# Collecting the 256-column side products of the composition at the end of each half of a group

## The reference, cut to what matters

```
x = x + L0(x, W0, b0, coeff, mask)          # x @ W0.T + b0 + coeff * (x @ (2*mask - 1))
x = x + L1(x, weight, ...)                  # x @ w_eff.T, w_eff a quantized 1024x1024 matrix
x = x + L2(x, W2, b2, lora_As, lora_Bs)     # x @ W2.T + b2 + 2 * (x @ A[tok2]) @ B[tok2]
x = x + L3(x, A3, B3)                       # (x @ B3[tok3].T) @ A3[tok3].T
```

## Time and profile before

| | us |
|---|---|
| median of 3 runs | 558.34 |
| profiled execution, its own time | 558.08 |
| span of the profile | 556.0 |
| around the span | 2.1 |
| PE busy | 541.1 |
| DVE busy | 397.4 |
| ACT busy | 330.4 |
| POOL busy | 151.2 |

### The profile page before, as it was taken

How to read it: one execution, slowest core, us unless ns; L and a number is a source line. 1 busy time by engine, 2 the same in 40 slices (tenths; PEclk the granted TensorE clock), 3 DMA queues, 4 the chain that set the end, 5 groups by cost and what they waited for, 6 DMA issues and landing times.

```text
span 556.0 us, 8879 instructions
## 1 busy us (share of the span) xinstructions
PE 541.1 (97%) x2892; PEld 464.4 (84%) x2892; DVE 397.4 (71%) x624; ACT 330.4 (59%) x624; POOL 151.2 (27%) x166
## 2 busy tenths in 40 slices
PE   5999999999998999999999999999999999999997
PEld 4988888888887888888888888888888888888886
DVE  5998898988856886585775767567576667856631
ACT  3777776776646765564565565546557556644620
POOL 2769778987710030021012002102100300210200
PEclk9999999999999999999999999999999999999999
DMA  8766042733686992481393367149138435814302
GB/s 230 242 90 145 21 141 70 238 107 109 122 200 220 280 259 90 150 209 72 129 204 130 132 144 215 59 156 233 56 138 186 154 130 133 227 39 151 75 0 75
DMA packets 138120, 80.07 MB, mean 144 GB/s; under 512 B 95664, under 2 KB 111024, under 8 KB 138096
## 3 DMA queue, kind: packets, MB, share of 16 engines
q1 hardware_dynamic: 137520, 78.71, 50.8%
q0 software_dynamic: 288, 1.05, 0.5%
q10 hardware_dynamic: 288, 0.01, 0.0%
HBM read 65.59 MB, written 14.16 MB: 143 GB/s over the span
## 4 chain that ended last, share of the span: by engine, by line
PE 83%; DVE 9%; ACT 3%; DMA 3%; issue 1%; POOL 0%; DVEq 0%; ACTq 0%; SPq 0%; POOLq 0%
PE bank L1406 19%; PE bank L1442 10%; PE bank L1443 10%; PE bank L1444 10%; PE bank L1413 10%; PE bank L1304 5%; PE bank L1306 5%; PE bank L1305 5%; PE bank L1455 3%; PE bank L1214 2%; PE bank L1462 1%; DVE w_lo L982 1%; ACT bank L567 1%; DVE merged_ring L1076 1%; PE bank L1228 1%; DVE m_lo L1082 1%
## 5 line engine op out<-in xcount | busy, mean ns | idle before, releaser
L1406 PE MATMUL bank<-x_t_pair,m_hi 128*128 128x512 f32 x512 | 128.5, 392 | 2.4 <-DVE P_lo L971 1.9
L733 ACT CAST m_hi<-merged_ring 128x512 fp32r<-128x512 f32 x128 | 73.1, 618 | 79.6 <-DVE merged_ring L1076 40.1
L1406 PEld LDWEIGHTS bank<-x_t_pair,m_hi 128*128 128x128 f32 x512 | 92.4, 189 | 20.0 <-DVE P_lo L971 2.3
L1082 DVE TENSOR_TENSOR m_lo<-merged_ring,m_hi 128x512 fp32r<-128x512 f32 x128 | 82.0, 687 | 34.8 <-ACT m_hi L733 34.8
L532 POOL TENSOR_TENSOR x_t_pair<-x_sum,x_t_pair 128x256 fp32r<-128x256 f32 x32 | 24.8, 804 | 283.5 <-ACT x_t_pair L778 283.5
L1442 PE MATMUL bank<-P_hi,x_t_pair 128*128 128x512 f32 x256 | 99.7, 389 | 0.0
L1443 PE MATMUL bank<-P_lo,x_t_pair 128*128 128x512 f32 x256 | 99.7, 389 | 0.0
L1444 PE MATMUL bank<-P_hi,x_t_pair 128*128 128x512 f32 x256 | 99.6, 389 | 0.0
L723 ACT ACTIVATE merged_ring<-mask_ring,batch_now 128x1024 f32<-128x1024 int32 x64 | 77.9, 1240 | 22.5 <-DMA mask_ring<-in_mask_Bx4096x_ik 21.7
L1076 DVE TENSOR_TENSOR merged_ring<-merged_ring,w_t 128x1024 f32<-128x1024 f32 x64 | 77.6, 1222 | 19.1 <-ACT merged_ring L723 17.3
L1413 PEld LDWEIGHTS bank<-x_t_pair,m_lo 128*128 128x128 f32 x512 | 69.8, 190 | 5.0
(11 more groups left out here) (151 smaller groups left out, 863.6 us busy)
## 6 DMA issues: line engine op xcount, KB each, us to landing
mask_ring<-in_mask_Bx4096x_ik SPq DMA_DIRECT2D x64, 512.0 KB, 4.9
out<-out_staged SPq DMA_DIRECT2D x32, 256.0 KB, 2.0
w_nat<-in_L_cond_W SPq DMA_DIRECT2D x14, 512.0 KB, 5.0
x_squares<-in_x SPq DMA_DIRECT2D x56, 128.0 KB, 3.1
w_raw<-in_L_cond_weight SPq DMA_DIRECT2D x16, 256.0 KB
g_batch<-g_dram SPq DMA_DIRECT2D x32, 128.0 KB, 2.8
w0t_dram<-w_out SPq DMA_DIRECT2D x14, 256.0 KB, 2.9
w_t<-w0t_dram SPq DMA_DIRECT2D x6, 512.0 KB, 5.2
```

What stands on the lines that cost most here:

```text
L733: nc.scalar.copy(Mh[:, n % MR], ring_f[:, k % MR, h * HALF:(h + 1) * HALF]).then_inc(s["h_set"], 1)
L1082: nc.vector.tensor_tensor(Ml[:, n % MR], ring_f[:, k % MR, h * HALF:(h + 1) * HALF], Mh[:, n % MR].bitcast(F32), ALU.subtract).then_inc(s[ ...
L1406: mm(bank[L0_BANK[HT * h + j]][:, :], Mh[:, n % MR, j * P:(j + 1) * P], xThl[:, k + i].rearrange("p i t -> p (i t)"), start=(k + i == 0), ...
```

## The change

The groups 0 to 6 no longer issue part 2 in each step. In steps 0 to 2 and 4 to 6 only parts 0 and 1 are issued (step 6: part 0 alone, as before); at the end of step 3 the side products of steps 0 to 3 stand in a row, and at the end of step 7 those of steps 4 to 7. The wait for bank 2 moves from step 0 to the end of step 3. The first half of group 0 already was so, and group 7 is as before. No instruction is added or removed; `delta`, the transposes and the rest keep their step t.

```diff
-                    if g == 0 and t < HT:
-
-                        comp(0, t, *w1_split(g))
-                        comp(1, t, *w1_split(g))
-                        if t == HT - 1:
-                            pe.wait_ge(s["v_lo"], 2)
-                            pe.wait_ge(s["ab_lo"], 1)
-                            for k in range(HT):
-                                comp(2, k, *w1_split(g))
-                                if k == 0:
-                                    b2_transpose(0)
+                    if g < G - 1:
+
+                        side_columns(g, t)
                         continue
...
+            def side_columns(g, t):
+                if t == 0 and g:
+                    pe.wait_ge(s["p_ready"], 3 * (g - 1) + 1)
+                comp(0, t, *w1_split(g))
+                if t == KT - 2:
+                    return
+                if t == 0 and g:
+                    pe.wait_ge(s["p_ready"], 3 * (g - 1) + 2)
+                if t == KT - 1:
+                    comp(1, t - 1, *w1_split(g))
+                comp(1, t, *w1_split(g))
+                if t % HT < HT - 1:
+                    return
+                if t == HT - 1 and g:
+                    pe.wait_ge(s["p_ready"], 3 * (g - 1) + 3)
+                elif t == HT - 1:
+                    pe.wait_ge(s["v_lo"], 2)
+                    pe.wait_ge(s["ab_lo"], 1)
+                for k in range(t + 1 - HT, t + 1):
+                    comp(2, k, *w1_split(g))
+                    if g == 0 and k == 0:
+                        b2_transpose(0)
```

## The result

| | before | changed |
|---|---|---|
| median of 22 runs each, us | 558.00 | 558.72 |
| ratio to before, 95% interval | | 1.0014, 1.0008 to 1.0020 |
| profiled execution, us | 558.08 | 558.63 |
| span, us | 556.0 | 556.6 |

The change makes the kernel slower by 0.14%: 0.78 us, between 0.45 and 1.1 (the ratio times 558.0). That lies within the 0.3% that the prediction called "no change", on the side that was forecast: +0.49 us, which is inside this interval, near its lower end. The forecast of 558.6 us meets the 558.72 better than it deserves: it was added to the 558.08 of the profiled execution, and from the median of 558.00 the same sum gives 558.5.

What follows compares the result with a forecast made beforehand. PE's own stream, busy 97% of the span, was taken as the bound. Terms +0.12 + 0.83 + 0.26 + 0.04 - 0.53 - 0.23 = +0.49 us on the profiled 558.08 gave 558.6 us, range 557.0 to 560.0.

Steps and rivals of the forecast that it cites:

- Price of a side product: PE's side matmuls: about 0.118 us each, 0.355 us per step in either order, so their sum does not change.
- rival 3: Long rows of side matmuls: weight loads no longer hide, 2.2 us on top, 560.8 us; chance 0.02.
- Group 0, +0.12: End of group 0: `delta` at t = 6 stays at 51.73, two side steps are owed; balance +0.12 us.
- Group 1, the main term, +0.83: Group 1: late `C_lo` delays `a3_transpose` by 0.45 us, two side products owed behind t = 7 transposes; +0.83 us.
- Group 2, +0.26: Group 2's transposes: late `gsum` delays `w0_evac` to 91.90, PE arrives at 91.70 and waits 0.26 us.
- Group 3, +0.04: Group 3's transposes: PE arrives at 101.39, may go at 101.43 behind ScalarE's L610; wait 0.04 us.
- Groups 4 and 5, 0: Groups 4 and 5: release moves with PE, 0 us; if wrong, one loan of 0.71 or 1.07 us.
- Borders, -0.53 and -0.23: Borders of groups 5/6 and 6/7: both waits for `P_lo` go, with 0.08 us restart each; -0.53 and -0.23 us.
- Group 7 and behind: Group 7 and the chain behind it: order unchanged, all moves with group 7, neither gain nor loss.
- only the waits go: Rival 1, group borders: three waits vanish and nothing is lost, -1.35 us, 556.7 us; chance 0.12.
- loans lost in full in groups 2 and 3: Rival 2, `w0_evac` in groups 2 and 3 late, PE idles for all it borrowed: +1.97 us, 560.1; chance 0.09.
- it does nothing: Rival 4, whole kernel: losses and gains cancel, group 1's side chains following `b2` and `a3` sooner; 558.1 us; chance 0.14.

Runs made afterwards that it cites:

- groups 1 to 6: Changed kernel with group 0 issued as in the kernel before: 557.93 us against 558.27 for the kernel before, ratio 0.9997.
- all but the first half of group 1: Changed kernel with the first half of group 1 interleaved as before: 558.92 us against 558.14 for the kernel before, ratio 1.0018.
- all but the second half of group 1: Changed kernel with the second half of group 1 interleaved as before: 558.90 us against 558.14 for the kernel before, ratio 1.0014.
- groups 0 to 2: Side products collected in groups 0, 1 and 2 only, rest as in the kernel before: 559.43 us against its 558.27, ratio 1.0022.
- 3 to 6: Side products collected in groups 3 to 6 only, rest as in the kernel before: 558.40 us against its 558.27, ratio 1.0007.
- 4 to 6: Side products collected in groups 4 to 6 only, rest as in the kernel before: 557.67 us against its 558.12, ratio 0.9992.
- 5 and 6: Side products collected in groups 5 and 6 only, rest as in the kernel before: 557.39 us against its 558.27, ratio 0.9985.
- second halves: Only side products of steps 4 and 5 of groups 5 and 6 moved, against the kernel before: 557.65 us against 558.12, ratio 0.9996.

## Why the prediction was right, point by point

- **Price of a side product: right.** 0.118 us in a row of twelve as in the earlier trace rows; rival 3, the weight loads, is refuted by that.
- **Group 0, +0.12 (start of group 1 at 57.35): right,** 57.35 with the 0.47 added. The wait for `P_lo` was covered, `delta` took its place, 0.94 us.
- **Group 1, the main term, +0.83: measured +0.76 (group 2 at +0.88, less the 0.12 of group 0), and right in its mechanism through `C_hi`, `C_lo`, the `a_t` copy and `bb`.** The wait at `a3_transpose` near 0.9 us is 0.87 from start to start, of which the profile shows 0.61 as idle. One more wait was not foreseen by name: for `delta` at t = 2 PE stands still for 0.18 us, until right behind VectorE's L944 (59.08 + 0.68 = 59.76), which comes 0.44 us late behind `C_lo`; with the 0.87 this makes the "microsecond" of the prediction. One sentence was wrong: that the transposes at t = 7 alone would cost 0.71 if `a3_transpose` did not. That anchor does not stand still, it hangs on `bb`: where `bb` comes 0.33 us sooner, L610 does too by 0.31 (groups 1 to 6), where it comes 0.48 later, L610 does by 0.48 (all but the first half of group 1). And PE, which has lost its time at `a3_transpose`, arrives behind it. Giving back the two owed side products ("all but the second half of group 1") gains nothing.
- **Group 2, +0.26: 0.32. Group 3, +0.04: 0.11. Groups 4 and 5, 0: 0.03 each.** `gsum` late by 0.87 (0.95 predicted) carried the loss on to L610, and the wait in group 2 is 0.26 us from start to start, as predicted. The missing 0.06 is a price that the prediction had for 512-column matmuls and not for transposes. Three pairs of rows show it, each the transposes and the matmul behind them. In the first (before, group 1, where PE has stood still for 0.22 us: 73.12 against 72.67 + 0.23) and the third (changed, group 2, with its wait of 0.26) it is 0.41 and 0.42 us from one to the other; in the second (before, group 2, without a wait) 0.35:

```profile
73.12 0.66 PE L1228 MATMUL bank<-ident,w_nat 128*128 128x128 f32 x4
73.53 0.47 PE L1304 MATMUL bank<-w_hi 128*128 128x512 f32 x1
...
91.46 0.60 PE L1228 MATMUL bank<-ident,w_nat 128*128 128x128 f32 x4
91.81 0.48 PE L1304 MATMUL bank<-w_hi,w_hi_early 128*128 128x512 f32 x1
...
91.41 0.66 PE L1228 MATMUL bank<-ident,w_nat 128*128 128x128 f32 x4
91.83 0.47 PE L1304 MATMUL bank<-w_hi,w_hi_early 128*128 128x512 f32 x1
```

The same 0.06 is saved in group 1, whose wait at t = 7 is gone, and paid in groups 2 and 3. The prediction saw nothing within half a microsecond in groups 4 and 5. For group 4 this holds only if the group ahead is collected too: as the first collected one, group 3 costs 0.85, group 4 0.44, group 5 only 0.03.

- **Borders, -0.53 and -0.23: -0.58 and -0.28.** Right, and the two parts that are worth having.
- **Group 7 and behind: moved with it.** The times can show this only within their intervals. Shift at the end of group 7, then the ratio as us: groups 0 to 2 +1.17 and +1.23; 1 to 6 +0.10 and -0.17; 3 to 6 +0.08 and +0.39; 4 to 6 -0.36 and -0.45; 5 and 6 -0.79 and -0.84; second halves -0.80 and -0.22; all but the second half of group 1 +0.51 and +0.78; all but the first +0.83 and +1.00. Each shift lies within the interval of its time.
- **Sum +0.49: 0.51 and 0.53 in the composition, 0.78 (0.45 to 1.1) in the times.** That the sum is met to 0.02 is partly luck: the terms were off by -0.07, +0.06, +0.07, +0.03, +0.03, -0.05 and -0.05, which nearly cancel. The rest, some 0.25 us, is within the interval. Whether the changed order adds a few tenths to the two loads behind group 7 is open; the prediction had no term for it.
- **Rivals.** 1 (only the waits go) and 2 (loans lost in full in groups 2 and 3) are ruled out by the table; rival 2's mechanism exists, in group 3, but at 0.85 us only where the group ahead is as before. 4 (it does nothing, since `bb` and what hangs on it come sooner): `bb` came 0.09 us later; the composition's +0.51 and +0.53 and the interval of the times rule it out.

## What to carry to other kernels

Where one engine bounds a stage and does others' chores at fixed places of its stream, moving its own work from ahead of such a place to behind it is a loan: look up, for each such place, when what it waits for is made, and whether that maker hangs on something that the move makes sooner. Collect work only directly ahead of the wait that it shall cover (here the last two side products of two groups), not everywhere: the same edit was worth -0.8 us in two groups and +1.3 in the rest. And count a loss at the first place where it bites, then work out anew when the engine arrives at the next: in group 1 the place at t = 7, which looked as tight, cost nothing more; in group 2 the transposes did.

## What the runs showed of the hardware that I had not expected

In some executions TensorE's granted clock falls to half shortly after PE has gone on from its wait of 1.6 to 2.0 us for `P_lo` at the start of the batches, and in others it does not. Five of the twelve profiles show the fall, with waits of 1.8 and 1.9 us, and seven do not, with waits of 1.6 to 2.0; so the length of the wait does not tell the two apart. Busy times by stretch of "groups 5 and 6" (us, then busy us of PE, PEld, DVE, ACT, POOL; granted clock, DMA share, GB/s):

```profile
174.00:176.00 2.00, 0.56 (x3) 0.13 (x1) 2.00 (x4) 1.49 (x3) 0.00 (x0) 1.00 0.54 119
176.00:178.00 2.00, 1.66 (x7) 1.38 (x8) 2.00 (x4) 2.00 (x5) 0.00 (x0) 0.85 1.01 372
178.00:180.00 2.00, 2.00 (x10) 1.90 (x10) 2.00 (x4) 1.27 (x4) 0.00 (x0) 0.50 0.92 299
180.00:182.00 2.00, 2.00 (x9) 1.59 (x8) 2.00 (x4) 0.44 (x1) 0.00 (x0) 0.80 0.93 326
182.00:184.00 2.00, 2.00 (x14) 1.82 (x13) 0.88 (x2) 1.04 (x2) 0.00 (x0) 1.00 1.06 409
```

0.50 is the lower of the two levels, 1.2 GHz. In the three stretches below 1.00 it was in force for 0.6, 2.0 and 0.8 us; the mean over the span is then 0.997, by which the runs without a profile can be sorted. Of the runs of the kernel before beside the experiments, 31 of 75 have a mean clock below 0.9985, with a median span of 556.5 us, and the other 44 have 555.8. In the changed kernel it is 9 of 22, 557.1 against 556.5. So the fall costs about 0.65 us in either kernel, as much as the change itself, and is as frequent in one (41%) as in the other (41%): it widens the times and does not explain their difference. Among the runs with the fall as among those without it, the changed kernel is 0.6 to 0.7 us longer.

3.4 us at half clock would cost 1.7 us of a full stream. Part of it is given back: from 184 to 200 us PE is busy for all 16.00 us in the five profiles with the fall, and for 14.9 to 15.5 us in the seven without. In the seven it waits there for `m_hi`, which is made from the masks; behind the fall it comes late enough not to. Whether the 0.65 us could be had back by giving PE work during the wait was not tried.
